# Joining a typed projection with the relation table it feeds, and storing the table's rows by index

## The reference

```python
k, q, v = (typed_linear(x, ntype, W) for W in (Wk, Wq, Wv))      # a 128x128 matrix per node type
kT = einsum('nhd,htdo->nhto', k, Watt)      # every node, every edge type: the relation table
vT = einsum('nhd,htdo->nhto', v, Wmsg)
a  = (kT[src, :, etype] * q[dst]).sum(-1) * pri[:, etype].T / 4
att = edge_softmax(a, dst)
hag = segment_sum(vT[src, :, etype] * att, dst)
h  = silu(typed_linear(hag, ntype, Wa))
h  = h * sigmoid(skip[ntype]) + x * (1 - sigmoid(skip[ntype]))
x  = layernorm(h) * g + b
```

## Time and profile before

| | before |
|---|---|
| median of 3 runs | 4091.22 us |
| profiled execution | 4095.23 us |
| its span | 4093.4 us |
| PE, DVE, ACT, POOL busy | 61%, 63%, 39%, 60% |
| moved by DMA | 804.87 MB, 197 GB/s |
| mean granted TensorE clock | 0.737 of full |

### The profile page before, as it was taken

How to read it: one execution, slowest core, us unless ns; L and a number is a source line. 1 busy time by engine, 2 the same in 40 slices (tenths; PEclk the granted TensorE clock), 3 DMA queues, 4 the chain that set the end, 5 groups by cost and what they waited for, 6 DMA issues and landing times. The chain is left out here.

```text
span 4093.4 us, 62881 instructions
## 1 busy us (share of the span) xinstructions
PE 2490.5 (61%) x13663; PEld 1768.1 (43%) x13664; DVE 2595.1 (63%) x6913; ACT 1587.2 (39%) x3599; POOL 2474.9 (60%) x2636
## 2 busy tenths in 40 slices
PE   0455666536666666666465656646666766666487
PEld 0222222225555555555342222225555555555465
DVE  6305556547777777777555556546777777777654
ACT  0115555513343334343334556523333343333332
POOL 3773333357777777775474333347777777777266
PEclk9867888857777777776677888866677777777555
DMA  3358999964444454444546999974455545444322
GB/s 78 114 125 346 423 414 412 417 199 136 136 135 138 132 138 133 137 133 134 113 125 251 424 414 414 417 281 137 133 137 133 138 134 135 134 135 126 81 71 54
DMA packets 305716, 804.87 MB, mean 197 GB/s; under 512 B 69459, under 2 KB 230048, under 8 KB 292894
## 3 DMA queue, kind: packets, MB, share of 16 engines
q1 hardware_dynamic: 189645, 545.43, 36.2%
q0 software_dynamic: 98384, 255.10, 22.5%
q10 hardware_dynamic: 17408, 1.08, 0.3%
HBM read 349.53 MB, written 460.43 MB: 198 GB/s over the span
## 5 line engine op out<-in xcount | busy, mean ns | idle before, releaser
L701 POOL DMA_INDIRECT region<-relation_table,key_of x1664 | 1632.9, 981 | 579.1 <-issue 504.1
L1027 PE MATMUL bank<-region,onehots 128*128 128x136 f32 x3328 | 729.7, 384 | 431.7 <-DVE region L1400 348.8
L1027 PEld LDWEIGHTS bank<-region,onehots 128*128 128x128 f32 x3328 | 621.5, 270 | 525.1 <-DVE sums L1415 290.0
L990 PE MATMUL bank<-region 128*128 128x512 bf16 x1568 | 519.1, 483 | 389.3 <-ACT region L813 314.1
L829 ACT ACTIVATE onehots<-iota_free,minus_dst 128x128 f32<-128x128 f32 x1664 | 528.7, 388 | 562.8 <-PE bank L1027 559.7
L1362 DVE COPY region<-bank 128x512 f32<-128x512 f32 x784 | 496.6, 684 | 380.8 <-DMA relation_table<-region 347.7
L1013 PE MATMUL bank<-region_q,onehotT 128*128 x4992 | 589.4, 275 | 93.0 <-DVE onehotT L1386 87.9
L1378 DVE TENSOR_TENSOR region<-bank,region 128x512 f32<-128x512 f32 x416 | 286.9, 690 | 514.1 <-DMA region<-relation_table,key_of 502.1
L1013 PEld LDWEIGHTS bank<-region_q,onehotT 128*128 128x128 bf16 x4992 | 502.2, 125 | 175.7 <-issue 114.3
L813 ACT COPY region<-bank 128x512 f32<-128x512 f32 x784 | 418.1, 602 | 373.4 <-DMA relation_table<-region 317.5
L1415 DVE TENSOR_TENSOR sums<-sums,bank 128x136 f32 x1664 | 473.4, 285 | 76.9 <-DVE sums L1415 46.5
(11 more groups left out here) (225 smaller groups left out, 2839.1 us busy)
## 6 DMA issues: line engine op xcount, KB each, us to landing
relation_table<-region SPq DMA_DIRECT2D x98, 4096.0 KB, 15.5
edge_places_in<-edge_places SPq DMA_DIRECT2D x416, 128.0 KB, 3.3
region<-relation_table,key_of POOLq DMA_INDIRECT x1664
sums<-qkv_rows SPq DMA_DIRECT2D x98, 192.0 KB, 15.4
flags<-segment_flags SPq DMA_DIRECT2D x104, 128.0 KB
region<-x_sorted SPq DMA_DIRECT2D x32, 256.0 KB, 2.9
aggregated_rows<-sums SPq DMA_DIRECT2D x6, 768.0 KB, 5.2
x_sorted<-region SPq DMA_DIRECT2D x16, 256.0 KB, 2.3
```

The costliest lines, as they stand in the source:

```text
L701: pool.indirect_dma_start(out=rows[:, block_.r, q * QUAD + s], out_offset=None, in_=table, in_offset=bass.IndirectOffsetOnAxis(ap=key_of[: ...
L990: nc.tensor.matmul(bank[2 + k % 6][:, :], x_spreadT[:, par, k, :], w_rel[:, k, :], start=True, stop=True).then_inc(table_psum, 1)
L1027: ins = nc.tensor.matmul(bank[SUM_BANK[q % 2][pair]][:, s * SUMC:(s + 1) * SUMC], onehots[:, at, 2 * pair + s], rows[:, block_.r, slot, RH ...
```

## The change

`typed(0)` with `build_table(0)`, and `typed(1)` with `build_table(1)`, become one loop `fused(l)` over the 64 sorted tiles; `typed(2)` becomes `finish()`. Step t of the loop works on several tiles: products and evictions of tile t, turning of the spread of tile t+1, POOL's split of t+2, the projection of t+3, and, in layer 2, the gate, sum and normalisation of the next groups in pieces by t mod 4.

q, k and v don't go through memory. ACT writes the three copies of the first 16-bit part out of PSUM, and q, k, v into a ring of four; POOL makes the rest from them with one copy and two subtractions. q goes by an indirect DMA to `q_rows` and is loaded as a whole and split after the table (by ACT and DVE, in four parts). The table's tile is stored by an indirect DMA from POOL with one row of 32 KB per node, the row number from `scatter_node`; empty places are out of bounds and not written. The products use four banks instead of six; ACT evicts nine heads, DVE seven and half of the turned spread. Group tiles and the edge stage's small tiles move to a new `arena`.

```diff
+IN_BANK, QKV_BANK, SPREAD_BANK, TABLE_BANK, TABLE_BANKS = 0, 1, (2, 3), 4, 4
+ACT_HEADS = [0, 2, 4, 6, 8, 10, 12, 14, 15]
 ...
@@ sync: before, in build_table
-                    sp.wait_ge(stage_act, c * H + (l * NTILES + 1) * H)
-                    sp.wait_ge(stage_dve, c * H + (l * NTILES + 1) * H)
-                    sp.dma_start(table[bass.ds(c * P * RT, P * RT), :].rearrange("(p t) n -> p t n", t=RT),
-                                 stage[:, k % 2]).then_inc(table_stored[k % 2], 16)
-                    if more:
-                        load(i + 1, k)
@@ sync: attend
+                for k in range(KV_RING):
+                    sp.wait_ge(q_scattered[k], 16 * (TILES // KV_RING) * (l + 1))
 ...
+                for k, part in enumerate(AGG_PARTS):
+                    sp.dma_start(q_stage[:, part], q_dram.rearrange("(c p) d -> p c d", p=P)[:, part]).then_inc(q_in[k], 16)
@@ gpsimd: fused
+            def split_kv(tile):
+                k = tile.k
+                pool.wait_ge(kvq_ready, l * TILES + tile.n + 1)
+                pool.wait_ge(upper_ready, l * TILES + tile.n + 1)
 ...
+                chain.step(nc.gpsimd.tensor_tensor(left, kv, spread[:, :, 0, :], ALU.subtract))
+                chain.wait()
+                chain.step(nc.gpsimd.tensor_copy(spread[:, :, 3:6, :], bc(left, 2, 3)))
+                chain.wait()
+                nc.gpsimd.tensor_tensor(spread[:, :, 6:8, :], bc(left, 2, 2), bc(spread[:, :, 3, :], 2, 2),
+                                        ALU.subtract).then_inc(spread_ready, 1)
+            def store_table(tile):
+                pool.wait_ge(stage_act, A * (l * TILES + tile.n + 1))
+                pool.wait_ge(stage_dve, V * (l * TILES + tile.n + 1))
+                pool.indirect_dma_start(out=table.rearrange("(n t) d -> n (t d)", t=RT),
+                                        out_offset=bass.IndirectOffsetOnAxis(ap=scatter_node[:, tile.n:tile.n + 1], axis=0),
+                                        in_=stage[:, tile.par].rearrange("p t n -> p (t n)"), in_offset=None,
+                                        bounds_check=N - 1, oob_is_err=False).then_inc(table_stored[tile.par], 16)
+            for at in range(-4 * GROUP, SORTED_TILES + 1):
+                tile = Tile(0, at)
+                if tile.shift(-1).real:
+                    store_table(tile.shift(-1))
+                if l and tile.j == 3 and 0 <= tile.g + 2 < GROUPS:
+                    power(tile.g + 2)
+                if tile.shift(2).real:
+                    split_kv(tile.shift(2))
+                    store_q(tile.shift(2))
+                coming = tile.shift((4 if l else 3) * GROUP)
+                if coming.real:
+                    gather_piece(coming)
@@ scalar: fused
+                def keep_qkv(tile):
+                    act.wait_ge(qkv_psum, tile.n + (l * TILES + 1))
 ...
+                    nc.scalar.copy(x_spread[:, tile.par, :, 0:3, :], bc(heads, 2, 3)).then_inc(upper_ready, 1)
+                    nc.scalar.copy(kvq[:, tile.k], bank[QKV_BANK][:, 0:3 * D]).then_inc(kvq_ready, 1)
+                def step(tile):
 ...
+                    if tile.real:
+                        evict(tile)
+                    if tile.j == 1 and group(1).real:
+                        turn_hn(group(1))
+                    if tile.shift(1).real:
+                        turn_spread(tile.shift(1))
+                    if tile.shift(3).real:
+                        keep_qkv(tile.shift(3))
+                    if not l:
+                        return
+                    if tile.j == 3 and group(3).real:
+                        turn_in(group(3))
+                    if tile.j == 0 and group(2).real:
+                        gate(group(2))
+                    if tile.j < 2 and group(2).real:
+                        scale_res(0, group(2).g, group(2).gpar, group(2).ghalf, (2 * tile.j, 2 * tile.j + 1))
@@ scalar: attend
+                for m in range(3):
+                    for k, part in enumerate(AGG_PARTS):
+                        if m == 0:
+                            act.wait_ge(q_in[k], 16 * (l + 1))
+                        else:
+                            act.wait_ge(q_left, 8 * l + 4 * m + k - 3)
+                        nc.scalar.copy(q_parts[:, part, m], q_stage[:, part].bitcast(BF16)[:, :, 1::2]).then_inc(q_copied, 1)
@@ tensor: fused
+                    if l == 0 and tile.first and tile.at == -1:
+                        for c in range(SCOLS):
+                            turn_slots(c)
+                    if l == 0 and tile.first and tile.at == 0:
+                        pe.wait_ge(w_rel_in, 16 * 2 * PARTS)
+                        pe.wait_ge(prep_done, 1)
 ...
+                    if tile.real:
+                        build(tile)
+                    if tile.j == 1 and group(1).real:
+                        turn_hn(group(1), tile)
+                    if spread.real:
+                        for half in ((1, 0) if tile.j == 1 else (0, 1)):
+                            turn_spread(spread, half)
+                    if new.real:
+                        project_qkv(new, new_types)
 ...
+                    if tile.j == 3 and group(3).real:
+                        turn_in(group(3))
+                    if tile.j == 0 and group(2).real:
+                        project_in(group(2), in_types)
@@ vector: attend
+                for m in range(2):
+                    for k, part in enumerate(AGG_PARTS):
+                        dve.wait_ge(q_copied, 12 * l + 4 * m + k + 1)
+                        v.tensor_tensor(q_stage[:, part], q_stage[:, part], q_stage[:, part].bitcast(BF16)[:, :, 1::2],
+                                        ALU.subtract).then_inc(q_left, 1)
+                dve.wait_ge(q_copied, 12 * (l + 1))
                 link(v.memset(sums[:, :, :], 0.0))
```

More of the change, by code:

```diff
@@ L57 @@
 Z_BANK, OUT_BANK = (1, 7), (3, 4)
+IN_BANK, QKV_BANK, SPREAD_BANK, TABLE_BANK, TABLE_BANKS = 0, 1, (2, 3), 4, 4
+KV_RING = 4
+ACT_HEADS = [0, 2, 4, 6, 8, 10, 12, 14, 15]
+DVE_HEADS = [k for k in range(2 * H) if k not in ACT_HEADS]
+LOOP_TURNS = 6
 SUM_BANK = ((5, 6), (7, 0))
@@ L380, in repeat, with __init__, shift, in_turn @@
                     chain.n = start + per * count
+        class Tile:
+            def __init__(self, turn, at):
+                self.turn, self.at, self.n = turn, at, 8 * turn + at
+                self.k, self.par, self.half = at % KV_RING, at % 2, 4 * turn + at // 2
+                self.j, self.g = at % GROUP, 2 * turn + at // GROUP
+                self.gpar, self.ghalf = (at // GROUP) % 2, turn + at // (2 * GROUP)
+                self.first = isinstance(turn, int)
+                self.real = not self.first or 0 <= self.n < SORTED_TILES
+            def shift(self, n):
+                return Tile(self.turn, self.at + n)
+        def in_turn(eng, step, chain=None):
+            for at in range(-4 * GROUP, 0):
+                step(Tile(0, at))
+            def turn(i):
+                for at in range(2 * GROUP):
+                    step(Tile(i, at))
+            repeat(eng, LOOP_TURNS, turn, chain)
+            for at in range(8 * LOOP_TURNS, SORTED_TILES):
+                step(Tile(0, at))
         def group_rows(array, g):
@@ L691, in attend @@
+                        gather(g + lead)
+                    if 0 <= g - 2 < GROUPS:
+                        scatter(g - 2)
+                    power(g)
             def attend(l):
                 for par in range(2):
-                    pool.wait_ge(table_stored[par], 16 * stage_uses(l + 1, 0, par))
+                    pool.wait_ge(table_stored[par], 16 * (TILES // 2) * (l + 1))
                 def gather(block_, q):
@@ new lines, in layer_constants, with scale_res @@
+            def layer_constants(l):
+                act.wait_ge(layer_const_in, 64 * (l + 1))
+                nc.scalar.activation(alpha_t[:, :], alpha_t[:, :], ACT.Exp, scale=-1.0).then_inc(alpha_exp, 1)
+            def scale_res(l, g, gpar, ghalf, tiles):
+                act.wait_ge(res_in[gpar], 16 * ghalf + (16 * l * HALF_GROUPS + 16))
+                act.wait_ge(layer_const_ready, l + 1)
+                for t in tiles:
+                    ins = nc.scalar.activation(g_res[:, gpar, t], g_res[:, gpar, t], ACT.Copy,
+                                               scale=one_less_alpha[:, bass.ds(g * GROUP + t, 1)])
+                ins.then_inc(res_scaled, 1)
@@ L797, in typed @@
                     groups(i)
[L798 to L821 removed]
+                normalise(HALF_GROUPS - 1, 1)
             def attend(l):
@@ L890, in turn_slots @@
                 nc.tensor.matmul(bank[7][0:1, 3 * P:4 * P], cross_col[:, c:c + 1], ident[:, :], start=True, stop=True)
[L891 to L902 removed]
+                nc.tensor.matmul(bank[6][0:1, 0:P], slot_dt[:, c:c + 1], ident[:, :], start=True, stop=True).then_inc(slot_T, 1)
@@ L999, in attend @@
+                for g in range(3):
+                    project(g // 2, g % 2)
+                repeat(pe, HALF_GROUPS - 2, groups)
```

(4 more changed lines are left out.)

722 lines of the change are left out of this document (373 added, 349 removed).

## The result

| | before | after |
|---|---|---|
| median of the runs | 4091.26 us (4 runs) | 4153.7 us (4 runs, 4150.39 to 4156.87) |
| ratio to before, 95% interval | | 1.0154 [1.0136, 1.0171] |
| span of the profiled run | 4093.4 us | 4155.0 us |
| layer 1: start to first table gather | 846.8 | 941.8 |
| layer 2: first aggregate gather to first table gather | 736.3 | 709.3 |

The change is slower by 62 us where I forecast 4032 and a gain. Layer 1's joined stretch lost 95.0 us. Layer 2's gained 27.0, the last stretch (table gather of layer 2 to the end) 5.0, and the edges of layer 1 took 1134.6 instead of 1136.0. 95.0 - 1.4 - 27.0 - 5.0 is 61.6, the difference of the spans, so the whole question is layer 1's stretch.

A forecast was written before the change was run, and what follows sets the result against it. Table writes bound the table stretches, POOL's issuing the edges. Joining projection and table gains 22 us in layer 1 and 37 in layer 2: 4095.2 becomes 4036, less 4.0 for the median, 4032 us; range 3890 to 4200.

The forecast's parts named there:

- What bounds the kernel, and what can be gained: Half-idle DMA projection stretches (176 and 205 us) precede all-DMA table stretches (535 and 531); joining them is the possible gain.
- the sum: Layer 1 to first table gather: 48 x 10.5 + 11 x 8.0 + 5 x 9.0, plus start and landing: 825 us.
- the cost of POOL: Joined loops: three DMAs at 1.28 us plus split work and gaps, 6.9 us a tile, leaving 3 us of slack.
- B: Joined loops compute-bound and slower, with PE granted less clock: 58 and 49 us worse, 4200; chance 0.19.
- C: Table store from POOL's queue slower, in transfer (250 us more a layer, 4540) or in issue (4290); chance 0.10.
- second form: Table store of 32 KB rows takes POOL 4 us more to issue, its step 12 us a tile: 4290.
- My 9.0 and 9.7 us: Joined loops: time of a compute-bound tile without a store to wait for, in layer 1 and layer 2.
- D: Joined loops: short stores overlap further, up to 520 us a layer at full rate; half of that gives 3910; chance 0.15.
- Unseen operations: Joined loops, operations absent from the earlier trace: DVE's 1024-wide copy 1.1 us, ACT's spread 0.8, POOL's 512-element subtraction 1.2.
- Layer 2: First aggregate gather to first table gather: 35 us serial run plus 664 us of loop, 699 against 736.3; gain 37.
- The rule against it: DVE work in SBUF delays POOL-issued DMAs, 0.7 us each; 20 us worse in layer 2 without POOL slack, so left out.
- The path of q, at nothing: After the table, q's copies and a memset start PE and DVE's edges some 20 us later, under 50 us of cover.

The follow-up runs named there:

- lead10: Changed kernel with POOL's gather of x in layer 1 moved two tiles later (10 tiles ahead instead of 12): 4045.87 us, ratio to before 0.9873.
- lead10_again: The lead10 kernel run again on the third chip: 4591.9 us, ratio to before 0.9857.

## Why the prediction was wrong

- *What bounds the kernel, and what can be gained*: right. With the gather two tiles later the first table gather came at 826.8 us, where the sum said 825. That it fits to 2 us is in part luck: the first product came at 174.3 instead of 180, the stretch from there took 652.5 us instead of 645, and a mean interval of 10.13 us (9.95 by the terms) holds the empty tiles that end the layer at 6.5 to 6.9 where I had 9.0, so the others took longer than their terms. The DMA share reached 0.84 and not over 0.9.
- *The failed step* is the cost of POOL, and the margin worked out from it: "an eviction starts when the store of two before has landed (1 us), lasts 5.8, POOL issues (1.3)", and "POOL has 3 us a tile". I priced POOL's gather at 1.28 us, as an issue, and summed its work, while the gather also waits for PE's turning of the group whose buffer it fills. The table store had moved from SP's queue, where nothing held it, to stand behind that wait. The prediction names no such wait, and none of its rivals is it: B and C, which end slower, have other causes. The busy sum itself was right: POOL's step without waits is 6.6 us, where I had 6.9. The runs put the wait at 115 us in layer 1 (109 in all), of 122 that the forecast missed by; most of the rest is layer 2's 10 us, below.
- *C, the indirect store*: false, as the prediction leaned. The argument from an issue of 0.98 us for rows of any size held, 0.99 for rows of 32 KB, and the rate, 402 GB/s, is the direct store's. (The sum of its second form was off: 6.9 + 4 is 10.9 us a tile, not 12, which gives some 4150 and not 4290.)
- *B, compute-bound*: false. The clock in the loop was 0.79, 0.86 in layer 2. My 9.0 and 9.7 us for a tile bound by the engines were too long: 7.8 and 8.2 without the writes, though with PE at 0.99; at the clock of the full loop PE is busy 7.0 us a tile (450.05/64) instead of 6.1 (391.79/64), still far from 10.3. Of ACT's 7.9, 7.0 was there, because copies that follow each other overlap: nine take 4.94 to 5.00 us, 0.55 each, and 0.60 is the length of one. The earlier trace rows had this already, 418.1 us for 784 copies, 0.53 each. Of the 1 us of waits for PE some 0.8 remained.
- *D, more hidden*: the loop of lead10 has a DMA share of 0.84; the 520 us of a full queue were never near. (By my own terms this was 136 us below the sum in layer 2, not 127.)
- *Unseen operations* (min/median/max ns): DVE's copy, ACT's spread, POOL's second subtraction.
```profile
L1419 DVE COPY region<-bank x128: 690/691/693, 174.7 to 2771.2; 128x1024 bf16<-128x1024 bf16 x128
...
L809 ACT CAST region<-bank x128: 798/799/839, 148.8 to 2758.1; 128x768 bf16<-128x768 f32 x128
...
L649 POOL TENSOR_TENSOR region<-sums,region x128: 1151/1153/1167, 170.0 to 2761.0; 128x512 bf16<-128x512 f32 x128
```
  I took 1.1, 0.8 and 1.2. DVE's was the lower bound.
- *Layer 2*: predicted 699, measured 709.3. The loop was right (mean interval 10.33 against 10.24 by my terms, though here too the empty tiles came at 6.5 to 6.9 where I had 9.7); the ramp to the first store took 51.1 and not 35 and one eviction, 41, because the gathers needed 16 us to the first turning where I had 8. The trace of before had this too, from the first gather at 1982.78:
```profile
1998.58 1.11 PE L911 MATMUL bank<-ident,region 128*128 128x128 f32 x4 [37.10 <-DMA region<-aggregated_rows,gather_node]
```
- *The rule against it*, left out: right. In layer 2, too, POOL's store still waited for ACT's copies (50 times, 171.0 us), so POOL had slack. But the earlier trace rows doesn't single out a two-port mode: DVE's fp32 subtractions and casts to bf16 alternate there.
- *The path of q, at nothing*: right. Start of layer 2's edges, after:
```profile
2785.72 0.99 POOL L729 DMA_INDIRECT region<-relation_table,key_of  x1 [6.44 <-issue]
...
2800.28 5.61 DVE L1722 MEMSET sums<- 128x6664 f32 x1 [3.92 <-issue]
...
2808.24 0.69 DVE L1565 TENSOR_TENSOR region<-bank,region 128x512 f32<-128x512 f32 x1 [1.68 <-PE bank L1139]
```
  DVE multiplies its first edges 22.5 us after POOL's first gather. In the kernel before it was 6.8 us, so the edges start some 16 us later, where I had some 20, and the edge stretch isn't longer: 1134.6.

## What to carry to other kernels

When an instruction is moved to another engine's queue, list the waits of everything that now stands ahead of it there, not only their durations, and follow each wait back: here it led through the very buffer that the delayed store was to free. A busy sum with slack (3 us a tile) says nothing of a wait in an in-order queue. Where two loops with the same bytes differ (layer 1 and 2 here), one long interval in each buffer group that only the slower loop has (20 to 24 us here) points at the prefetch distance; a lead that is *too long* asks for a buffer that isn't free yet, and shortening it by two tiles turned a ratio of 1.015 into 0.987.

## What the runs showed of the hardware

An indirect store from POOL with 32 KB rows runs at the rate of a direct one (402 and 404 GB/s) and takes 1.0 us to issue. Beside DVE's fp32 subtraction in SBUF, POOL's gathers took longer to issue, as the earlier trace rows had hinted:
```profile
2787.66 8.70 DVE L1719 TENSOR_TENSOR sums<-sums 128x1664 f32<-128x1664 f32 x5 [1.96 <-ACT region_q L928]
2788.30 2.08 POOL L729 DMA_INDIRECT region<-relation_table,key_of  x1 [0.30 <-issue]
2790.69 1.36 POOL L729 DMA_INDIRECT region<-relation_table,key_of  x1 [0.30 <-issue]
...
2798.74 0.95 POOL L729 DMA_INDIRECT region<-relation_table,key_of  x1 [0.30 <-issue]
```
That is 2.08 and four times 1.36 to 1.50 us against 0.95, 3 us in all. The Trainium skill (SBUF — State Buffer, "Who interferes with whom") says that `tensor_tensor` has no two-port mode, but with both inputs in SBUF contends with GpSimd's reads. The trace agrees that such an operation delays POOL, by 0.4 to 1.1 us a gather; whether it is the read of the index that waits is not shown. And one chip is not another: with equal instruction times on POOL, DVE and ACT the edge stretch took 1136 us on the first and 1395 to 1421 on the other two, in which POOL, the bound before, waited besides. In lead10_again L729 waited 303.7 us (126 times) for something that the trace calls remote, tied to no queue it knows, and 203.2 us for PE's sums, L1153; in lead10 it was none and 3.4 us. The cause stays open.
